# Output weights in four quadrants of the array, and another split of the first stage's rows between ScalarE and VectorE

## The reference

```python
x = x + attn(layernorm(x), w_qkv, w_conv, w_fc, b_fc)
x = x + ffn(layernorm(x), router_w, w_gate, w_up, w_down)

# attn, per batch and head
q_l, k_l = mean of q, k over 16 neighbouring rows        # 64 landmarks
out = softmax(q k_l^T) @ pinv6(softmax(q_l k_l^T)) @ (softmax(q_l k^T) @ v)
out = out + conv13(out)                                   # 13 taps along the rows, one filter per head
out = concat(heads) @ w_fc + b_fc
```

## Time and profile before

| | |
|---|---|
| median of 3 runs | 1186.02 us (1185.68 to 1186.12) |
| the profiled execution | 1188.56 us, its span 1186.8 us |
| mean granted TensorE clock | 0.991 |
| TensorE busy | 1122.7 us, 95% of the span |
| VectorE busy | 571.7 us, 48% |
| ScalarE busy | 301.7 us, 25% |
| GpSimd busy | 301.8 us, 25% |

### The profile page before, as it was taken

One profiled execution on the slowest core, in us unless ns is written; L12 is line 12 of the kernel. 1 busy time (PEld: TensorE's weight loads), 2 busy tenths in 40 slices (PEclk: granted clock), 3 DMA queues, 4 the chain that ended last, 5 costly groups with the idle time before them and its releaser, 6 DMA issues.

```text
span 1186.8 us, 22648 instructions
## 1 busy us (share of the span) xinstructions
PE 1122.7 (95%) x9066; PEld 886.9 (75%) x9066; DVE 571.7 (48%) x1273; ACT 301.7 (25%) x513; POOL 301.8 (25%) x298
## 2 busy tenths in 40 slices
PE   3999999999987899999999999878999999999997
PEld 3866667666776756677767766767888888899996
DVE  6254243232256557667777676654233323334442
ACT  4532222222223423223332332321111111111110
POOL 6000000000020003225435534443322332234343
PEclk9999999999999999999999999889999999999999
DMA  9300000000210030312321213235223332221221
GB/s 334 135 1 1 1 1 1 1 1 1 55 40 5 4 142 10 108 50 68 117 82 63 99 60 124 85 99 145 45 48 52 50 49 48 43 41 38 45 23 15
DMA packets 48551, 69.12 MB, mean 58 GB/s; under 512 B 7872, under 2 KB 41792, under 8 KB 47424
## 3 DMA queue, kind: packets, MB, share of 16 engines
q1 hardware_dynamic: 34720, 47.50, 12.5%
q0 software_dynamic: 13296, 16.92, 8.1%
q10 hardware_dynamic: 432, 3.24, 0.7%
HBM read 42.10 MB, written 26.46 MB: 58 GB/s over the span
## 4 chain that ended last, share of the span: by engine, by line
PE 89%; DVE 4%; issue 3%; POOL 1%; ACT 1%; another core or an unknown queue 1%; POOLq 0%; DVEq 0%; ACTq 0%
PE ps L1585 20%; PE ps L1608 10%; PE ps L1470 10%; PE ps L1268 9%; PE ps L1248 9%; PE ps L1509 9%; PE ps L1501 5%; PE ps L1259 3%; PE ps L1382 2%; PE ps L1211 1%; PE ps L1568 1%; PE ps L1489 1%; PE ps L1455 1%; PE ps L1223 1%
## 5 line engine op out<-in xcount | busy, mean ns | idle before, releaser
L1585 PE MATMUL ps<-mem 128*128 128x256 f32 (+1 forms) x1504 | 260.4, 329 | 0.0
L1585 PEld LDWEIGHTS ps<-mem 128*128 128x128 f32 x1504 | 232.6, 191 | 21.3
L554 POOL DMA_INDIRECT out<-mem x71 | 124.6, 1755 | 253.8 <-DVE mem L1130 188.0
L1608 PE MATMUL ps<-mem 128*128 x568 | 137.2, 385 | 5.0 <-DVE mem L1122 3.4
L524 POOL TENSOR_TENSOR mem<-mem,small 128x1024 f32<-128x1024 f32 x36 | 68.6, 1904 | 248.9 <-DVE small L1059 115.9
L1470 PE MATMUL ps<-mem 128*128 128x512 f32 x288 | 129.7, 594 | 1.3 <-DVE mem L943 1.3
L1122 DVE TENSOR_TENSOR mem<-mem,ps 128x512 f32<-128x512 f32 x71 | 48.8, 687 | 170.5 <-PE ps L1585 143.1
L742 ACT ACTIVATE mem<-ps 128x512 f32<-128x512 f32 x71 | 42.4, 597 | 322.6 <-PE ps L1585 315.8
L1509 PE MATMUL ps<-mem 128*128 128x256 f32 x512 | 119.7, 387 | 0.0
L1608 PEld LDWEIGHTS ps<-mem 128*128 128x128 f32 x568 | 105.6, 193 | 18.3 <-issue 5.7
L1248 PE MATMUL ps<-mem 128*128 128x512 f32 x256 | 115.4, 593 | 0.0
(11 more groups left out here) (205 smaller groups left out, 1316.2 us busy)
## 6 DMA issues: line engine op xcount, KB each, us to landing
mem<-w_gu SPq DMA_DIRECT2D x9, 1024.0 KB, 4.3
mem<-xs_d SPq DMA_DIRECT2D x22, 260.0 KB, 2.9
mem<-x SPq DMA_DIRECT2D x8, 512.0 KB, 7.4
mem<-x SPq DMA_DIRECT2D x32, 128.0 KB, 2.2
out<-mem SPq DMA_DIRECT2D x32, 128.0 KB, 1.7
mem<-w_down SPq DMA_DIRECT2D x8, 512.0 KB, 5.7
xnt_d<-mem ACTq DMA_DIRECT2D x3, 1056.0 KB, 4.4
mem<-xnt_d SPq DMA_DIRECT2D x3, 1056.0 KB, 4.9
```

Of the source, the lines that this page charges most:

```text
L554: pool.indirect_dma_start(out=out_rows, out_offset=bass.IndirectOffsetOnAxis(ap=rows[:, D + 1:D + 2].bitcast(U32), axis=0), in_=ys[:, r % ...
L1585: mm = pe.matmul(bank(2 * c + n % 2)[:, i * size:(i + 1) * size], w[:, k, c, f * P:(f + 1) * P], xst[:, a % 2, k, 0:size], start=(k == 0), ...
L1608: mm = pe.matmul(bank(down_bank(a, b))[:, 0:D], hid[:, u, i * size + b * P:i * size + (b + 1) * P], w_d_s[:, e, f], start=(f == 0), stop=( ...
```

## The change

There are five edits. `ACT_ROWS` becomes one tuple for each batch: (3, 5, 7), (3, 5, 7), (7), and none; the waits count accordingly. ScalarE executes one small activation at its start. The last chunk of the last batch is copied out by VectorE. The four pairs of a group alternate between the quadrants with equal halves and the crossed ones, in two banks, and VectorE's copy into `pm` puts them in order; for odd pairs the two heads then stand on exchanged halves. The convolution writes its heads to match: column halves 0, 1, 1, 0, 0, 1, 1, 0, ... in place of 0, 1, 0, 1, ...

```diff
-ACT_ROWS = (2, 5, 7)
+ACT_ROWS = ((3, 5, 7), (3, 5, 7), (7,), ())
+def act_rows(b, until=0):
+    return sum(len(rows) for rows in ACT_ROWS[:b]) + sum(t < until for t in ACT_ROWS[min(b, B - 1)])
+def dve_rows(b, until=0):
+    return RT * b + until - act_rows(b, until)
...
-            sp.wait_ge(s("a_xn_dve"), (RT - len(ACT_ROWS)) * (B - 1))
-            sp.wait_ge(s("a_xn_act"), len(ACT_ROWS) * (B - 1))
+            sp.wait_ge(s("a_xn_dve"), dve_rows(B - 1))
+            sp.wait_ge(s("a_xn_act"), act_rows(B - 1))
...
             act.wait_ge(s("a_consts"), 1)
+            act.activation(zz[:, 6:7], ident[:, 0:1], ACT.Identity, bias=ident[:, 1:2], scale=ident[:, 2:3])
...
-                for t in ACT_ROWS:
+                for t in ACT_ROWS[b]:
...
                 for n, ts in enumerate(CHUNKS):
+                    if b == B - 1 and n == len(CHUNKS) - 1:
+                        act.wait_ge(s("a_xnt_dve"), 2 * KD)
+                        continue
...
-                    act.wait_ge(s("a_xnt"), 12 * (b + 1))
+                    act.wait_ge(s("a_xnt"), 12 * (b + 1) - (2 * KD if b == B - 1 else 0))
...
-                    if t not in ACT_ROWS:
+                    if t not in ACT_ROWS[b]:
...
             normalise(B - 1)
+            ts = CHUNKS[-1]
+            for k in range(KD):
+                c = 6 * B - KD + k
+                dve.wait_ge(s("a_tp"), c + 1)
+                product = bank(c % 8)[:, 0:len(ts) * (P + RT)].rearrange("p (t c) -> p t c", t=len(ts))
+                at_ = HALO + P * ts[0]
+                dve.tensor_copy(xnts[B - 1][:, k, at_:at_ + P * len(ts)].rearrange("p (t c) -> p t c", t=len(ts)),
+                                product[:, :, 0:P]).then_inc(s("a_xnt_dve"), 1)
+                lm = M * (B - 1) + RT * ts[0]
+                dve.tensor_copy(xm[:, k, lm:lm + RT * len(ts)].rearrange("p (t c) -> p t c", t=len(ts)),
+                                product[:, :, P:P + RT]).then_inc(s("a_xnt_dve"), 1)
...
-                dve.tensor_copy(pm[:, g // 2, 4 * (g % 2):4 * (g % 2) + 4],
-                                bank(2 + 2 * (g % 2), 2).rearrange("p (s c) -> p s c", s=4)).then_inc(s("p_pm"), 1)
+                dve.tensor_copy(pm[:, g // 2, 4 * (g % 2):4 * (g % 2) + 4].rearrange("p (s o) c -> p o s c", o=2),
+                                bank(2 + 2 * (g % 2), 2).rearrange("p (o s c) -> p o s c", o=2, s=2)).then_inc(s("p_pm"), 1)
...
-            pe.wait_ge(s("a_xnt"), 12 * B)
+            pe.wait_ge(s("a_xnt"), 12 * B - 2 * KD)
+            pe.wait_ge(s("a_xnt_dve"), 2 * KD)
...
                     q = 4 * g + i
-                    for r in halves:
-                        mm = pe.matmul(bank(2 + 2 * (g % 2), 2)[r, i * D:(i + 1) * D], wts[r, g % 2, i], wfc[r, q % J],
-                                       start=True, stop=True)
+                    to = bank(2 + 2 * (g % 2) + i % 2)[:, i // 2 * D:(i // 2 + 1) * D]
+                    for h, r in enumerate(halves):
+                        mm = pe.matmul(to[halves[(h + i) % 2]], wts[r, g % 2, i], wfc[r, q % J], start=True, stop=True)
...
                 for h in range(H):
-                    c = 64 * (h % 2)
+                    c = 64 * ((h + h // 2) % 2)
```

More of the change, by code:

```diff
@@ L1203, in _ @@
                 for n, ts in enumerate(CHUNKS):
-                    pe.wait_ge(s("a_xn_dve"), (RT - len(ACT_ROWS)) * b + sum(t not in ACT_ROWS and t <= ts[-1] for t in range(RT)))
-                    pe.wait_ge(s("a_xn_act"), len(ACT_ROWS) * b + sum(t <= ts[-1] for t in ACT_ROWS))
+                    pe.wait_ge(s("a_xn_dve"), dve_rows(b, ts[-1] + 1))
+                    if act_rows(b, ts[-1] + 1):
+                        pe.wait_ge(s("a_xn_act"), act_rows(b, ts[-1] + 1))
                     for k in range(KD):
```

## The result

The changed kernel takes 1175.97 us (median of 7 runs, 1171.41 to 1180.73), the kernel before 1186.02 (7 runs beside them, 1183.47 to 1189.38). The ratio is 0.9921, 95% interval 0.9894 to 0.9948: faster by 0.8%, forecast 1174.7 against 1176.0. The profiled execution is the fastest of the seven: 1171.41, span 1169.7. Between the two profiled executions lie 17.1 us, between the medians 10.05, so the stretches have to be read one by one.

A forecast was written before the change was run, and what follows sets the result against it. TensorE's program order was taken as the bound, with idle time between first-stage batches. First stage 4.5 plus quadrants 6.8 plus convolution 0 gave 11.3 us, so 1186.0 became 1174.7; forecast itself 1172 to 1177, full range 1171.5 to 1181.6.

The forecast's parts named there:

- The rule on banks: Output stage: different row tiles cannot access one bank at once, so L1455's pairs would run one behind the other.
- Rival A: Output stage: crossed quadrants bring nothing at 256 columns because two quadrants share a path; 1181.5 us, chance 7%.
- rival D: Output stage: VectorE or ScalarE bounds the new group at 3.0 instead of 2.56 us; 1178.0 us, chance 8%.
- Rival B: Convolution: products start in strict program order, costing 1.7 us in all; time 1176.4 us, chance 15%.
- rival C: Convolution: weight loads behind a waiting product are not drawn ahead, costing 24.7 us; time 1199.4 us, chance 5%.
- the row at 350.47: Pseudo-inverse trace: a crossed pass starts 0.03 us ahead of products preceding it in program order, cited for the convolution costing 0.
- The count of cycles: Convolution: 8 products per column half at 2 x 116 cycles each; 116 cycles at 2.4 GHz taken as 0.097 us.
- the ends of the tail: First stage's end: VectorE's last copies end at about 34.45 us, TensorE goes on at 34.5, a gain of 4.5.
- step (c): First stage, batch 2: VectorE's seven tiles are ready in time, so the batch runs from 25.6 to 29.55 us.
- the last condition: Sign of being wrong: the time saved in the two stages is given back between 740 and 830 us.

The follow-up runs named there:

- the two part kernels: The kernel before with only the first stage's edits, 1183.85 us, and with only the four quadrants and the convolution order that goes with them, 1178.27 us.
- the blocks of four: The changed kernel with the convolution's 16 products issued four for one column half, four for the other, and again; its one run took 1189.53 us.

## Why the prediction was right

**The four quadrants.** 8 x 0.85 = 6.8 was forecast, 6.85 measured, and the same 6.85 between 26.62 and 19.77 in the two part kernels. Passes, group (2.54, forecast 2.56) and VectorE's spare time came as worked out. The step that carried it was the reading of the earlier trace rows, that crossed quadrants cost almost nothing beside the equal ones; it holds for 256 columns as for 64. The rule on banks that the prediction sets against it did not hold here: both row halves write eight passes into each bank, which one behind another would take 8 x 0.216 = 1.73 us, and all sixteen took 1.09. Rival A and rival D are refuted by the 1.09 and the 2.54.

**The convolution.** Forecast 0, measured 0.00. The reason was right in kind and is now bounded: quadrants run apart by one waiting product. Rival B's 1.7 and rival C's 24.7 are refuted; the blocks of four show what an order that asks for more would cost. The rule quoted from the Trainium skill (TensorE: Matmul & The Clock Gate, The mechanism), strict program order of matmuls, does not hold in these runs: in the blocks of four, the first product of the second half starts with the third of the four before it, and the fourth, which also precedes it in the program, starts later. It was this run that showed it, not the row at 350.47. Equal and crossed products alternate there in the program, so the L1366 passes at 350.50 can belong to the pair behind the crossed product, and the row fits strict order too. The forecast of 0 rested on a weaker ground than the prediction says.

The count of cycles there and ahead of it is wrong by a factor of two, without effect on the sum. The prices come from measured spacings: a pass every 0.099 us for 116 columns, every 0.216 for 256, at a granted clock of 1.00. At 2.4 GHz these are 238 and 518 cycles, two per moving column and not one; 116 cycles would be 0.048 us.

**The first stage.** 4.5 forecast, 4.43 measured, and the ends of the tail within 0.05 (34.5 and 34.54). The steps inside were less exact. Batch 0 ended at about 20.1, sooner than the 21.6 that I took: the copies of the changed kernel come 1.36 us apart at first and 0.69 apart from 18.7 on, so its passes left the half rate earlier than in the first profile of the kernel before. Batch 1 ended at 24.4 and not at 25.6, and batch 2 did not follow at once, as step (c) has it, but waited for VectorE's first tiles. None of this mattered, because batches 2 and 3 wait for VectorE and GpSimd (the 1.10 and 0.44 above); the projections start at 34.5 to 34.6 behind a slow first batch too. In the kernel before it does matter. Its two later profiles, TensorE's rows:

```profile
15.63 5.78 PE L1211 MATMUL ps<-ids,mem 128*128 128x136 f32 x32 [15.63 <-ACT mem L579]
...
38.13 3.07 PE L1223 MATMUL ps<-mem 128*128 128x256 f32 x13 [0.55 <-ACT mem L592]
```

```profile
15.69 6.92 PE L1211 MATMUL ps<-ids,mem 128*128 128x136 f32 x32 [15.69 <-ACT mem L579]
...
39.33 1.99 PE L1223 MATMUL ps<-mem 128*128 128x256 f32 x8 [0.55 <-ACT mem L592]
```

Batch 0 takes 5.78, 6.62 or 6.92, and all that follows moves with it: 38.13, 38.97, 39.33. The kernel with the quadrants alone, whose first stage is unchanged, fits in with 5.60 and 38.02; that is why it missed my 38.97. In the changed kernel the projections start at 34.54 and 34.63. The gain of this part is therefore 3.4 to 4.8, depending on the execution, and that the first pair of profiles shows 4.43, so close to 4.5, is in part luck. Two edits that I listed as steps, the early table load and VectorE's tail, add nothing to the tiles; the tiles alone bring the gain, the start at 14.8 included.

**The sum.** 11.3 was forecast and 10.05 measured between the medians, with an interval of some 3 us either way. Between the first token steps of the two profiles it is 10.12, and 11.3 without the 1.18 of the pseudo-inverse. Since one stretch can differ by 5 us between executions, the stretches test the sum better than the medians do. Rivals A to D are settled by their own rows; the last condition, that time is given back between 740 and 830, did not come about: the stretch was shorter, if anything.

## What to carry to other kernels

Where products have 64 rows and 64 columns of weights and their results may stand on either half, issue them in turn to all four quadrants, the equal and the crossed ones in two banks; check that the engine which copies them out has the time. In the three orders tried here, the order of products over quadrants or column halves was free as long as no more than one had to wait in any of them. When engines share a stage, give an engine tiles only as far as its whole round (tiles, copies, stores) stays below TensorE's, and give it those that the first chunk does not need; and take each helping edit back alone before keeping it: here the tail and the early load carried nothing beside the tiles. An edit can also be worth something only in some executions, as the fewer tiles behind a slow first batch; one profile of each kernel does not show that.

## What the runs showed of the hardware

- A column half can lag behind the program order by one waiting product: in the blocks of four, the other half starts when two of the four products are done, where a strict order would let it start only after the fourth had begun. Cost of that order: 0.56 us a convolution (2.37 against 1.81).
- Four quadrants with 256 fp32 columns each run at once at the pace of two: 16 passes in 1.09 us in place of 1.94, written to two banks. The passes start by fours, 0.216 us apart. Row halves wrote to one bank at the same time throughout, in different partition halves. The same bank and the same partitions from both row halves was not tried.
- The moment at which TensorE leaves the half rate after its idle start shifts from execution to execution of one kernel: its first 32 passes took 5.78, 6.62 and 6.92 us. With the moment the full rate sets in, ScalarE's copies of their products go from 1.36 to 0.69 us apart in the changed kernel, while the granted clock of that window reads 1.00.
- An fp32 pass takes two cycles of the 2.4 GHz clock per moving column (0.216 us for 256 columns, 0.116 for 136, 0.099 for 116), in a quadrant or column half as in the whole array.
- One kernel can take 111.07 or 106.35 us for one stretch of its program without a change in it. The two profiles are from two chips; the long length goes with a wait of ScalarE of 6.3 to 9.8 us in all six profiles that have it.
